# TensorE's order in one attention step: the long part of the scores between the two parts of the transposition

## What is computed

```python
q = layernorm(x)                                   # 8 x 224 x 2048
scores = einsum('bsgrd,btgd->bgrst', q, ctx) / 8 + mask    # t: 750 context rows
probs = softmax(scores)
out = einsum('bgrst,btgd->bsgrd', probs, ctx)
x = x + tanh(g_xattn) * out
x = x + tanh(g_ffn) * ffn(layernorm(x))
```

## Time and profile before

| | us |
|---|---|
| median of 3 runs | 1288.43 |
| the profiled execution, its own time | 1289.38 |
| its span, first to last instruction | 1287.6 |
| TensorE matmuls busy in the span | 1189.3 (92%) |
| VectorE busy | 983.7 (76%) |
| ScalarE busy | 894.4 (69%) |
| GpSimd busy | 893.9 (69%) |

### The profile page before, as it was taken

The page is one execution under the profiler, slowest core; times in us unless marked ns, Lnnn a source line. Parts: engine busy times, 40 slices in busy tenths (PEclk is TensorE's granted clock), DMA queues, the critical chain, the costliest instruction groups (busy, mean ns, idle before and its releaser), DMA issues.

```text
span 1287.6 us, 34874 instructions
## 1 busy us (share of the span) xinstructions
PE 1189.3 (92%) x14357; PEld 921.2 (72%) x14608; DVE 983.7 (76%) x2206; ACT 894.4 (69%) x1221; POOL 893.9 (69%) x845
## 2 busy tenths in 40 slices
PE   1999999999999999999999999999799998999985
PEld 0888888888888888888888888888475554444442
DVE  3897898899889889988988988888647774555543
ACT  2888888888888888888888888888214345334332
POOL 1899999999999998999999999999200013322221
PEclk9999999999999999999999999999799998999998
DMA  7312222132131213213122211220362000112112
GB/s 265 129 51 72 59 82 72 45 99 78 38 97 41 77 52 92 72 50 93 38 83 57 75 50 45 63 56 15 93 240 101 1 1 1 66 66 86 78 66 98
DMA packets 60080, 94.68 MB, mean 74 GB/s; under 512 B 35666, under 2 KB 44882, under 8 KB 55572
## 3 DMA queue, kind: packets, MB, share of 16 engines
q1 hardware_dynamic: 59492, 89.86, 22.0%
q10 hardware_dynamic: 432, 2.59, 0.5%
HBM read 71.35 MB, written 20.97 MB: 72 GB/s over the span
## 4 chain that ended last, share of the span: by engine, by line
PE 76%; ACT 9%; POOL 5%; DVE 5%; issue 2%; DMA 2%; SPq 0%; POOLq 0%; DVEq 0%
PE psum L744 12%; PE psum L721 11%; PE psum L841 10%; PE psum L751 7%; PE psum L732 6%; PE psum L774 5%; PE psum L768 5%; PE psum L769 5%; PE psum L825 4%; POOL arena L502 4%; PE psum L784 2%; PE psum L853 2%; PE psum L703 2%; ACT arena L607 2%; ACT arena L603 2%
## 5 line engine op out<-in xcount | busy, mean ns | idle before, releaser
L502 POOL TENSOR_TENSOR arena<-arena 128x768 bf16<-128x768 f32 x448 | 651.4, 1467 | 62.2 <-ACT arena L603 43.1
L994 DVE CUSTOM_DVE_ANT_0 arena<-psum,arena 128x750 f32<-128x750 f32 x448 | 420.2, 938 | 99.2 <-PE psum L732 91.1
L607 ACT ACTIVATE arena<-arena,neg_max 128x750 f32<-128x750 f32 x448 | 411.0, 917 | 59.8 <-DVE neg_max L994 59.7
L603 ACT ACTIVATE arena<-psum 128x768 f32<-128x768 f32 x320 | 258.0, 806 | 69.5 <-PE psum L751 67.3
L744 PE MATMUL psum<-ident,arena 128*128 128x128 f32 x1792 | 268.4, 272 | 0.0
L721 PE MATMUL psum<-arena 128*128 128x512 bf16 x675 | 222.1, 383 | 15.7 <-DVE arena L1009 1.6
L768 PEld LDWEIGHTS psum<-arena 128*128 128x128 bf16 (+1 forms) x2688 | 195.3, 98 | 57.4
L769 PE MATMUL psum<-arena 128*128 128x64 bf16 (+1 forms) x2688 | 222.6, 193 | 0.0
L768 PE MATMUL psum<-arena 128*128 128x65 bf16 (+1 forms) x2688 | 222.3, 194 | 0.0
L769 PEld LDWEIGHTS psum<-arena 128*128 128x128 bf16 (+1 forms) x2688 | 179.1, 98 | 53.2
L744 PEld LDWEIGHTS psum<-ident,arena 128*128 128x128 f32 x1792 | 206.0, 140 | 4.4
(11 more groups left out here) (133 smaller groups left out, 1387.4 us busy)
## 6 DMA issues: line engine op xcount, KB each, us to landing
arena<-in_k_t SPq DMA_DIRECT2D x128, 187.5 KB, 3.3
out<-arena SPq DMA_DIRECT2D x14, 1024.0 KB, 3.8
arena<-in_v_rows SPq DMA_DIRECT2D x64, 192.0 KB, 2.4
arena<-in_x_top SPq DMA_DIRECT2D x7, 1024.0 KB, 6.5
arena<-in_x_rest SPq DMA_DIRECT2D x8, 768.0 KB, 4.8
spill<-arena SPq DMA_DIRECT2D x96, 64.0 KB, 2.2
arena<-spill SPq DMA_DIRECT2D x6, 1024.0 KB, 8.4
arena<-in_w_t SPq DMA_DIRECT2D x4, 1024.0 KB, 13.1
```

What stands on the lines that cost most here:

```text
L502: pool.tensor_tensor(p_lo[:, n % RING, :], p_sb[:, n % RING, :], high(p_sb[:, n % RING, :]), ALU.subtract).then_inc(p_split, 1)
L603: act.activation(p_sb[:, n % RING, :], flat_ps[:, turned_at(n):turned_at(n) + CW], ACT.Copy).then_inc(evac_a, 1)
L607: act.activation(s_sb[:, n % RING, 0:CTX], s_sb[:, n % RING, 0:CTX], ACT.Exp, bias=neg_max[:, n % 4, :], scale=-1.0).then_inc(exped, 1)
L994: dve.tensor_tensor_reduce(s_sb[:, n % RING, 0:CTX], flat_ps[:, score_at(n):score_at(n) + CTX], mask_sb[:, max(n % UNITS - REP + 1, 0), :] ...
```

## The change

In TensorE's step, `score_main(k + 5)` moves from behind `turn_mid(k + 2)` to before it. Before the order is turn_main, turn_mid, score_main, value, score_mid; afterwards it is turn_main, score_main, turn_mid, value, score_mid. All waits and signals move with their functions. No other engine's list changes.

```diff
                 if 0 <= k + 2 < NU:
                     turn_main(k + 2)
-                    turn_mid(k + 2)
                 if 0 <= k + 5 < NU:
                     score_main(k + 5)
+                if 0 <= k + 2 < NU:
+                    turn_mid(k + 2)
                 if k >= NU - 2:
                     turn_h(0, k - (NU - 2))
                 if k >= 0:
```

## The result

The changed kernel takes 1294.58 us (median of 16 runs, 1291.85 to 1298.18), the kernel before 1291.04 in the same number of runs. The ratio of their mean times is 1.0033, with a 95% interval of 1.0022 to 1.0043: 4.3 us slower, where the medians differ by 3.5. I had forecast 4.7, inside the interval's 2.8 to 5.6. The profiled execution has a span of 1294.7 us, 7.1 more than before, and only part of that is the change. From the first load of T to that of unit 440 the attention takes 865.8 us against 861.4, so +4.5; the start came 0.7 later, and the feed-forward part behind it, which the change doesn't touch, took 1.9 more.

A forecast was written before the change was run, and what follows sets the result against it. TensorE was taken as the bound, its matmuls busy 848.5 of 870 us. +3.4 us net through ScalarE and VectorE plus +1.3 through GpSimd made +4.7, a median of 1293.1 us; range for 8 in 10, 1287.5 to 1297.

The forecast's parts named there:

- The switch between kinds: TensorE's alternation of transpositions and score matmuls in the new order: zero cost, with 4.4 us either way kept for the range.
- The gain, 5.5 us: At the end of windows 1 to 3, turn_mid no longer waits for VectorE's copy: 5.5 us over seven batches.
- The price through ScalarE to VectorE: Later `turned` delays ScalarE's queries copy and VectorE's maximum, so score_mid waits in windows 1 to 3: +3.4 us net.
- GpSimd, +1.3 us: GpSimd's split chain starts 0.45 us later, lengthening TensorE's waits around window 5 in the first three batches: +1.3 us.
- ScalarE in window 5: ScalarE's normalisation chain and turn_mid both come 0.45 us later, so the wait stays unchanged: zero.
- Undisturbed windows: Windows where score_mid has 0.48 us margin after VectorE's maximum; the shift takes 0.45 or less: nothing lost, but only just.
- The sum: Net +3.4 us through VectorE plus +1.3 us through GpSimd: +4.7 us, a median of 1293.1 us.
- Rival A: VectorE's remainder isn't tied to ScalarE, so turn_mid's waits vanish without a price: -5.5 us, 1282.9 us; chance 0.14.
- Rival B: Gain and price cancel through slack in VectorE or GpSimd: 0 to 2.5 us, say 1289 us; chance 0.19.
- Rival C: VectorE's copy waits for `turned`, so score_mid loses 0.1 us in about 40 further windows: +4 on top, 1297; chance 0.12.
- D: The change doesn't do what it says on TensorE; the prediction saw no way to it and gave no chance.

The follow-up runs named there:

- e3: Changed kernel, with ScalarE's copy of the queries put ahead of its copy of unit m6 in the step at m4; ratio 0.992.
- e6: Kernel before, old TensorE order, with ScalarE's copy of the queries put ahead of its copy of unit m6 at m4; ratio 0.9954.
- e1: Kernel before, with the new order in only one of seven steps, the one at m4; ratio 1.0173.
- e4: Changed kernel, with VectorE's statistics of the remaining rows moved from m5 to m2, from the second batch on; ratio 0.9969.
- e9: Changed kernel, with GpSimd's weight slices kept out of windows 5, 13 and 21; one run, attention 863.2 us.
- e10: Kernel before, with GpSimd's weight slices kept out of windows 5, 13 and 21; one run, attention 860.2 us.
- e8: Changed kernel, with the queries' copy first at m4, statistics at m2 and normalisations at m3 to m5 of window 5; ratio 0.9917.
- e11: As e8, with GpSimd's weight slices also kept out of windows 5, 13 and 21; ratio 0.9897.
- e2: Kernel before, with the new order in six of seven steps and the old one at m4; ratio 0.9965.

## Why the prediction was right

- *The switch between kinds costs nothing*: right. T takes 0.44 us ahead of S as it did ahead of t, and the undisturbed windows are equal to 0.01 us.
- *The gain, 5.5 us*: right. 21 waits of t are gone. With the chain cut, e3 against e6, the three windows give back 7 x 0.78 = 5.5.
- *The price through ScalarE to VectorE, 0.41 at s, net +0.16, +0.17, +0.16*: right. The windows grew by 0.15, 0.17 and 0.15, in sum 0.47 a batch against 0.49. In the window shown the step of the late s takes 2.26, 0.40 over 1.86. e1 isolates the step, e3 cuts at the queries, e4 takes the statistics out. There was a little luck in the size: I took 0.45 for the delay of the maximum and 0.04 off at s; measured, the delay is 0.41 and next to nothing comes off at s (its margin was 0.07 us and is 0.06).
- *GpSimd, +1.3 us*: right. 0.44 in the second batch, zero in the sixth; e9 and e10 show that it hangs on the extra slice.
- *ScalarE in window 5, "the wait stays as it is"*: the time is right, 28.23 and 28.22 us, the mechanism only in part. Of the three places where t waits there, the second and third are as I said: t's load stands 0.42 and 0.45 later in its step, and the steps take 2.55 and 2.35, as before to 0.01. The first, the one in rows 9, isn't. Around it, first before and then after the change:

```profile
665.47 0.46 PEld L744 LDWEIGHTS psum<-ident,arena 128*128 128x128 f32 x4
...
667.76 0.46 PEld L744 LDWEIGHTS psum<-ident,arena 128*128 128x128 f32 x4
```

```profile
670.28 0.24 PEld L774 LDWEIGHTS psum<-arena 128*128 128x128 bf16 x6 [0.36 <-POOL arena L502]
...
670.60 0.46 PEld L744 LDWEIGHTS psum<-ident,arena 128*128 128x128 f32 x4
671.03 0.21 PEld L721 LDWEIGHTS psum<-arena 128*128 128x128 bf16 x2
671.50 0.22 PEld L751 LDWEIGHTS psum<-ident,arena 128*128 128x128 f32 x2 [0.26 <-ACT arena L603]
...
672.46 0.46 PEld L744 LDWEIGHTS psum<-ident,arena 128*128 128x128 f32 x4
```

  That step took 2.29 us and takes 1.86 now, although t's load stands 0.90 behind T's in both. In exchange the two steps before it are 0.44 longer, since the low part of the value product waits for GpSimd's split. My paragraph on GpSimd had this exchange ("the wait on ScalarE that follows takes them in"), the one on ScalarE contradicted it; both came to zero.
- *Undisturbed windows, nothing lost, only just*: right. The margin of s came down from 0.48 to 0.12, of which 0.05 is the reaction.
- *The sum*: 4.7 us forecast, 4.5 in the attention of the traces, 4.3 by the ratio. In the traces it is 3.2 after the statistics and 1.3 in windows 5 and 6; the very first window took 0.2 off, but it varies from 12.97 to 13.49 us between the traces of this study, also between kernels with one order.
- *Rival A* needed a path that isn't tied to ScalarE. There is none: VectorE idles 0.45 at the remainder. *Rival B* fell with the windows. *Rival C's* condition came true, since VectorE's copy of m5 does wait for `turned` now (63 places), but the windows didn't grow: the smallest margin left to s in undisturbed windows is 0.12. D had no chance by the code, and the timeline agrees.

Two readings in it were weak. "No other engine comes near it" was too strong: GpSimd is busy for 810.1 of the 870 us, and once the other waits are gone (e8, e11) it is the engine for which TensorE still waits in window 5. And I took the 21.5 idle us of TensorE as idle. In the same stretch the changed kernel shows TensorE busy for 855.7 us, 7 more than before though it is slower. The page of before lists 675 matmuls at L721, that of after all 896. Missing records look like idle time, here probably several us. The weight loads were complete in both (14608), and the argument rested on them.

## What to carry to other kernels

An instruction that is moved ahead of a waiting one fills its gap, but it also delays the signal that the waiting one gives. Follow that signal through every engine's list, to the first place with idle time of its own and from there back to the bound engine: where no idle time takes it up, it can cost more than the gap did (here 0.41 us against 0.25). In a loop whose steps differ, the same move can be good in some steps and bad in one, so decide step by step, and check the place where old and new order meet, where two of the moved instructions stand closer together than a step.

## What the runs showed of the hardware

- A weight load stands about one matmul ahead of its own, so how much a late load costs depends on what streams before it. Behind a 128-column transposition t's load leads its matmul by 0.11 us; there a load 0.11 late cost 0.06 of the step (e2), and one 0.29 late cost 0.25. Behind a 512-column matmul it leads by 0.22; there t's load at 671.50, shown above, was 0.13 late (0.47 behind that of S, where 0.34 is usual) and cost nothing: the step takes 1.86.
- Transpositions in float32 and matmuls in bf16 alternate without a gap on TensorE, in either order, at a granted clock of 1.00: the last transposition of T takes 0.11 us from its start to the next, whether a transposition or a score matmul follows.
